# A gated state-space block and a ternary MLP on one core: in VectorE's order the gated chunk of an MLP tile goes behind the scan of its slot

## The chip, the cores and the metric

The kernel runs on one core of a Trainium2 chip. The metric is device time in microseconds, of one launch from start to end. Below, PE is the matrix engine (TensorE), DVE is VectorE, ACT is ScalarE, POOL is GpSimd and SP is the engine that only issues DMAs here. Each engine works through its own list of instructions in the order in which they are written; between engines the order is kept by semaphores alone.

## The reference, cut to what matters

The input x has 4 batches of 512 rows of 512 numbers. Two blocks follow one another, both with a residual.

1. A state-space block. A projection of a context, a convolution along time and a projection give, for each of 512 channels d, inputs `u`, step sizes `dt` (softplus), and for 16 states rows `B` and `C`. The recurrence is `state = state * exp(dt * A) + (dt * u) * B` along the 512 time steps, and `y = sum over states of state * C + D * u`. Then `y` is multiplied by `silu` of the normalised x, scaled, and added to x.
2. A ternary MLP on the normalised result: `h = silu(x w1) * (x w2)`, `out = h w3`, in which each product takes activations quantised row by row to 8 bits (after a division by their root mean square) and weights rounded to -1, 0 and 1. Hidden width 2048. The result is scaled and added.

The loop at issue works on both blocks at once: it scans the states of one batch while the MLP works on rows that are already finished.

## The kernel before, in words

**The scan pipeline.** The work on the states is cut into 128 steps k: 4 batches, 32 steps each, and in each step 1024 columns for 128 channels (two states of 512 time steps, or, in batches 2 and 3, four states of 256 time steps). A step passes five stations:

- POOL multiplies `dt * u` by the rows of B into a buffer `hh[k % 6]` (`times_b`, L702 or L708).
- ACT makes `exp(dt * A)` into the PSUM pair `dbank[k % 2]` (`exp`, L736 or L743).
- DVE scans (`scan`, L773, or four pieces with a carried state, L770).
- POOL multiplies the states by the rows of C, in place (`times_c`, L813 or L818). In 11 steps (the list `BY_VECTOR`) DVE does this (L796).
- PE turns the result and adds it into the bank `bank_y` (`sums`, L851), which frees `hh[k % 6]` for step k + 6.

Slot k of the loop is written out per engine: in slot k POOL does `times_c(k)` and `times_b(k + 4)`, ACT `exp(k + 4)`, DVE `scan(k + 3)`, PE `sums(k - 1)`. `times_b(k + 4)` waits until PE has done `sums(k - 2)`. Every eighth slot (40, 48, ..., 120) a bank of y is complete, and DVE does `gate` (L576, and L585 or L591): it multiplies `bank_y` by the gate and adds x. `gate` in slot k waits for `sums(k - 1)`.

**The MLP between.** 16 tiles of 128 rows. Tile i starts in slot T = `TILE[i]`, most of them 6 slots apart (38, 44, 50, 56, 70, 76, 82, 88, 94, 100, 106, 112, 118 for the 13 tiles inside the loops), and has four chunks c of 512 hidden columns:

- PE in slot T + c: `a_tensor` (L1020) into `bank_a`, then `b_tensor` (L1029) into `bank_b`, four products each. There is one bank of either kind, so the products of chunk c wait until DVE has read the banks of chunk c - 1 (L1018 and L1027).
- ACT in slot T + c + 1: `tanh_scalar` (L1041) of the first bank, ahead of the slot's `exp`.
- DVE in slot T + c + 1: `gated_vector`, two instructions: (tanh + 1) times `bank_a` (L1048, marked `g`), and that times `bank_b` (L1054, marked `h`).
- ACT in slots T + 2 and T + 4: `square_scalar` (L1059 to L1068), waits for `h` of chunks 1 and 3. DVE in the same slots: `peak_vector` (L1093), the largest magnitude of two chunks.
- Later: scales (L1106 to L1116), quantising on ACT, turning on PE, and in slot T + 10 the third product (`out_tensor`, L1211, 16 products) and DVE's `out_vector` (L1218), which adds it to the rows and lets SP store them. With tiles 6 slots apart, slot T + 10 of one tile is slot T + 4 of the next.

**The gate's own input.** `silu` of the normalised x is made in `z_scalar` on ACT (L523 and L524, in two halves for batches 2 and 3) and `z_vector` on DVE (L530), in the slots 42, 48, 54, 68, 74, 80, 86, 98, 104, 110 and 117 (`z_slot`). `z_scalar` uses `bank_a` and waits for `g` of chunk 3 of the tile before; it stands behind `square_scalar` in ACT's list. Nine of these slots (all but 68 and 117) are slot T + 4 of a tile.

**The two loops.** DVE's list is written by a loop over slots 38 to 79 (L1868) and another over 80 to 124 (L1910). Their orders in a slot, before the change: in the first, scales of a tile (L1871), `gated_vector`, `gate`, `scan`, the product by C where it is DVE's, and the rest; in the second, scales, `gate`, statistics of finished rows, `gated_vector`, `scan`, and the rest. In both, `peak_vector`, `out_vector` and `z_vector` come behind, in this order.

Of the kernel before, what the change touches and what calls it, by code (L numbers as in the profile page):

```python
# [25 lines left out]
STEPS = NS // GN  # L26
PER = NE * STEPS
ALL = NB * PER
NH = 6
LEAD = 4  # L30
# [63 lines left out]
def build(nc, book, x, ctx_t, in_w, xp_w, dt_w, weights, consts, out):  # L94
    u_dram = nc.dram_tensor("u_scratch", [NB, P, NE, L], F32).ap()
    xd_dram = nc.dram_tensor("xd_scratch", [NB, ROWS, L], F32).ap()
    with ExitStack() as ctx:
# [474 lines left out]
        def gate(v, g):  # L572
            b, q = g // NE, g % NE
            v.wait_ge(s_sum, STEPS * (g + 1))
            v.wait_ge(*ZA.of(("gT", g)))
            YV.did(v.tensor_tensor(bank_y[:, :], bank_y[:, :], gbuf[:, q, :], ALU.mult))  # L576
            if b in SPLIT:
                h, p = q // 2, q % 2
                if p == 0:
                    for t in (2 * h, 2 * h + 1):  # L580
                        v.wait_ge(*d_out[t].of(NE * (b - 2) + t))
                v.wait_ge(*YV.now())
                to, rows = [of[:, 2 * h:2 * h + 2, 2 * p * P:2 * (p + 1) * P].rearrange("p c (j d) -> p j c d", j=2)
                            for of in (x2[b % 2], xin)]
                YV.did(v.tensor_tensor(to, bank_y[:, :].rearrange("p (j c d) -> p j c d", j=2, c=2), rows, ALU.add),  # L585
                       ("y", g))
                return
            if g == NE:
                v.wait_ge(*WA.of(("sign", NW - 1)))
            v.wait_ge(*YV.now())  # L590
            YV.did(v.tensor_tensor(columns(x2[b % 2], q), by_rows(bank_y[:, :]), columns(xin, q), ALU.add), ("y", g))  # L591
# [166 lines left out]
        def scan(v, k):  # L758
            if k < 2:
                v.wait_ge(*BV.of(2 * k + 1))  # L760
            else:
                v.wait_ge(s_m1, m1_done(k))
            v.wait_ge(s_exp, k + 1)
            h, da = flat(hh[k % NH]), flat(dbank[k % 2])
            to = da if c_by_vector(k) else h
            if split(k) and where_split(k)[1]:
                b, _, q, n = where_split(k)
                for j in range(4):
                    t = slice(HALF * j, HALF * (j + 1))
                    ins = v.tensor_tensor_scan(to[:, t], da[:, t], h[:, t], hl[:, q, n + j:n + j + 1],  # L770
                                               ALU.mult, ALU.add)
            else:
                ins = v.tensor_tensor_scan(to, da, h, 0.0, ALU.mult, ALU.add)  # L773
            ins.then_inc(s_scan, 1)
# [324 lines left out]
        def scales_vector(v, i, part):  # L1099
            t = i % NE  # L1100
            if part == 0:
                v.wait_ge(*MV.of(("peak", i, NCH - 1 if at_end(i) else 1)))
                if at_end(i):
                    MV.did(v.tensor_scalar(am1, amh[:, 0:1], amh[:, 1:2], amh[:, 2:3], ALU.max, ALU.max))
                else:
                    MV.did(v.tensor_scalar(am1, amh[:, 0:1], amh[:, 1:2], None, ALU.max))  # L1106
                v.wait_ge(*MV.now())
                MV.did(v.reciprocal(ram1, am1))
            if part == 1:
                v.wait_ge(*MG.of(("rh", i)))  # L1110
                v.wait_ge(*MV.now())
                MV.did(v.tensor_scalar(rk_most, rh, kk[:, t:t + 1], 127e5, ALU.mult, ALU.mult))
                MV.did(v.tensor_scalar(rk_am, rh, kk[:, t:t + 1], am1, ALU.mult, ALU.mult))
                v.wait_ge(*MV.now())
                MV.did(v.tensor_scalar(csh, ram1, 127.0, rk_most, ALU.mult, ALU.min), ("csh", i))
                MV.did(v.tensor_scalar(fin[i % 2], rk_am, 1e-5, g3d, ALU.max, ALU.mult), ("fin", i))  # L1116
                v.wait_ge(*MV.now())
# [111 lines left out]
        with nc.Block() as block:  # L1229
# [556 lines left out]
            def _(v):  # L1786
# [81 lines left out]
                for k in range(38, 80):  # L1868
                    for i in range(END):
                        if k == tile_slot(i) + 7:  # L1870
                            scales_vector(v, i, 1)  # L1871
                    for i in range(END):
                        c = k - tile_slot(i) - 1
                        if 0 <= c < NCH:
                            gated_vector(v, i, c)
                    if k % STEPS == 0 and PER < k <= ALL:
                        gate(v, k // STEPS - 1)
                    if k + LEAD - 1 < ALL:
                        scan(v, k + LEAD - 1)
                    if k + LEAD - 1 < ALL and c_by_vector(k + LEAD - 1):  # L1880
                        times_c_vector(v, k + LEAD - 1)
                    for first, n, done in TURNS:
                        if k == done + 3:
                            rows_vector(v, first, n)
                    for i in range(END):
                        if k == tile_slot(i) + 5:
                            scales_vector(v, i, 0)
                    for first, n, done in TURNS:
                        if k == done + 2:
                            for i in range(first, first + n):  # L1890
                                stats_vector(v, i)
                            for i in range(first, first + n):
                                aggr_vector(v, i)
                    for i in range(END):
                        if k == tile_slot(i) + 4:
                            peak_vector(v, i, 1)
                    for i in range(END - 1):
                        if k == tile_slot(i) + 10:
                            out_vector(v, i)
                    for i in TILES:  # L1900
                        if k == z_slot(i):
                            z_vector(v, i)
                    for n in PAIR:
                        if k == PAIR[n]:
                            du_vector(v, 2 * n)
                            du_vector(v, 2 * n + 1)
                    for i in range(END):
                        if k == tile_slot(i) + 2:
                            peak_vector(v, i, 0)
                for k in range(80, SLOTS):  # L1910
                    for i in range(END):
                        if k == tile_slot(i) + 7:
                            scales_vector(v, i, 1)
                    if k % STEPS == 0 and PER < k <= ALL:
                        gate(v, k // STEPS - 1)
                    for first, n, done in TURNS:
                        if k == done + 2:
                            for i in range(first, first + n):
                                stats_vector(v, i)
                            for i in range(first, first + n):  # L1920
                                aggr_vector(v, i)
                    for i in range(END):
                        c = k - tile_slot(i) - 1
                        if 0 <= c < NCH:
                            gated_vector(v, i, c)
                    if k + LEAD - 1 < ALL:
                        scan(v, k + LEAD - 1)
                    for i in range(END):
                        if k == tile_slot(i) + 5:
                            scales_vector(v, i, 0)  # L1930
                    for first, n, done in TURNS:
                        if k == done + 3:
                            rows_vector(v, first, n)
                    for i in range(END):
                        if k == tile_slot(i) + 4:
                            peak_vector(v, i, 1)
                    for i in range(END):
                        if k == tile_slot(i) + 2:
                            peak_vector(v, i, 0)
                    for i in range(END - 1):  # L1940
                        if k == tile_slot(i) + 10:
                            out_vector(v, i)
                    for i in TILES:
                        if k == z_slot(i):
                            z_vector(v, i)
                    for n in PAIR:
                        if k == PAIR[n]:
                            du_vector(v, 2 * n)
                            du_vector(v, 2 * n + 1)
                    if k + LEAD - 1 < ALL and c_by_vector(k + LEAD - 1):  # L1950
                        times_c_vector(v, k + LEAD - 1)
# [81 lines left out]
```

## Time and profile before

| | |
|---|---|
| median of 3 runs | 653.23 us (653.22 to 656.8) |
| profiled execution | 653.69 us, span 651.9 us |
| PE busy, instructions | 488.3 us (75%), 2560 |
| DVE busy, instructions | 583.0 us (89%), 772 |
| ACT busy, instructions | 530.7 us (81%), 969 |
| POOL busy, instructions | 587.9 us (90%), 289 |
| mean granted PE clock | 0.897 of full speed |
| chain that ended last | POOL 30%, DVE 29%, ACT 14%, issue 13%, PE 11%, DMA 2% |

The span is the time from the first to the last instruction of the profiled execution; its own time is 1.8 us longer. Busy shares are means over the whole span, in which the loop with MLP tiles runs from about 215 us to about 605 us. The chain that ended last is followed back from the last instruction: at each step to what released it, or to the instruction before it on its engine. "Issue" is time in which the engine waited for nothing that the profile shows.

### The profile page before, as it was taken

What the parts mean: (1) busy time and instruction counts of PE and PEld (TensorE: products, weight loads), DVE (VectorE), ACT (ScalarE), POOL (GpSimd) and SP (SyncE); (2) the same over time, 40 slices, a digit from 0 to 9 for tenths busy, and PEclk for the clock granted to TensorE, in tenths of its full rate; (3) what the DMA queues carried; (4) which work ended last, traced back from release to release, by engine and by line L of the source; (5) the groups of instructions that cost most, each with busy time, mean ns of one, the idle gap of its engine ahead of it and who ended that gap; (6) DMA issues with size and microseconds to landing.
All of it is one profiled execution on the core that took longest, in us unless ns stands there. A gap on an engine that the chain in (4) does not pass through costs nothing.

```text
span 651.9 us, 7928 instructions
## 1 busy us (share of the span) xinstructions
PE 488.3 (75%) x2560; PEld 296.4 (45%) x2560; DVE 583.0 (89%) x772; ACT 530.7 (81%) x969; POOL 587.9 (90%) x289
## 2 busy tenths in 40 slices
PE   8798878994564678777666486778676887668987
PEld 3254434552553445455534354455454554345543
DVE  6779779997998899999999999989997999999765
ACT  5764767788999778987798797899999898897675
POOL 1399999998999999999999999999999999999431
PEclk9988999997555979999786889889989897978999
DMA  5598587579960100147420100037700000000001
GB/s 186 193 407 309 183 329 276 198 270 389 374 262 0 39 1 2 47 153 276 132 78 0 33 2 17 1 127 244 254 37 1 17 1 18 0 16 18 1 17 48
DMA packets 24472, 80.77 MB, mean 124 GB/s; under 512 B 2464, under 2 KB 5152, under 8 KB 21360
## 3 DMA queue, kind: packets, MB, share of 16 engines
q1 hardware_dynamic: 24432, 80.27, 33.9%
q8 instruction: 20, 0.33, 0.2%
q14 instruction: 20, 0.16, 0.1%
HBM read 72.53 MB, written 7.73 MB: 123 GB/s over the span
## 4 chain that ended last, share of the span: by engine, by line
POOL 30%; DVE 29%; ACT 14%; issue 13%; PE 11%; DMA 2%; SPq 0%; DVEq 0%; POOLq 0%; ACTq 0%
POOL hh L708 15%; POOL hh L818 14%; DVE hh L773 9%; DVE hh L770 8%; DVE room L1048 4%; ACT da L736 3%; DVE sm L1093 2%; PE bank_a L1020 2%; PE bank_b L1029 2%; PE bank_y L851 2%; ACT room L1041 1%; PE da L1211 1%; DVE bank_y L576 1%; DVE sm L904 1%; ACT gbuf L922 1%
## 5 line engine op out<-in xcount | busy, mean ns | idle before, releaser
L773 DVE TENSOR_TENSOR_SCAN hh<-da,hh 128x1024 f32<-128x1024 f32 x85 | 193.4, 2280 | 3.1 <-ACT da L743 3.0
L851 PE MATMUL bank_y<-ident,hh 128*128 128x128 f32 x1024 | 145.3, 292 | 10.8 <-POOL hh L818 8.8
L851 PEld LDWEIGHTS bank_y<-ident,hh 128*128 128x128 f32 x1024 | 129.6, 152 | 40.1 <-issue 17.5
L813 POOL TENSOR_TENSOR hh<-hh,cc 128x1024 f32<-128x1024 f32 x60 | 141.0, 2350 | 0.2 <-ACT hl L756 0.2
L818 POOL TENSOR_TENSOR hh<-hh,cc 128x1024 f32<-128x1024 f32 x57 | 134.2, 2355 | 0.0
L708 POOL TENSOR_TENSOR hh<-pair,bb 128x1024 f32<-128x1024 f32 x30 | 70.5, 2352 | 26.4 <-DMA bb<-xd_scratch 24.2
L770 DVE TENSOR_TENSOR_SCAN hh<-da,hl,hh 128x256 f32<-128x256 f32 x128 | 85.4, 729 | 0.0
L708 POOL TENSOR_TENSOR hh<-wq,bb 128x1024 f32<-128x1024 f32 x32 | 75.3, 2357 | 1.8 <-PE bank_y L851 1.8
L702 POOL TENSOR_TENSOR hh<-wq,bb 128x1024 f32<-128x1024 f32 x32 | 75.1, 2346 | 0.3 <-PE bank_y L851 0.3
L702 POOL TENSOR_TENSOR hh<-pair,bb 128x1024 f32<-128x1024 f32 x32 | 75.2, 2355 | 0.0
L736 ACT ACTIVATE da<-wq,cst 128x256 f32<-128x256 f32 x128 | 53.3, 463 | 12.0 <-DVE hh L770 11.6
L743 ACT ACTIVATE da<-pair,cst 128x511 f32<-128x511 f32 x64 | 41.3, 679 | 23.3 <-DVE hh L773 23.3
L1020 PE MATMUL bank_a<-wq,room 128*128 128x512 fp8e4 x120 | 34.2, 412 | 30.2 <-DVE room L1048 27.4
L736 ACT ACTIVATE da<-pair,cst 128x255 f32<-128x255 f32 x128 | 53.0, 459 | 3.5 <-DVE hh L773 3.4
L743 ACT ACTIVATE da<-wq,cst 128x511 f32<-128x511 f32 x64 | 41.4, 682 | 9.4 <-DVE hh L773 9.2
L1020 PE MATMUL bank_a<-wq,xqT 128*128 128x512 fp8e4 x112 | 32.4, 417 | 21.7 <-DVE room L1048 21.7
L1041 ACT ACTIVATE room<-bank_a,sm 128x512 f32<-128x512 f32 x58 | 39.0, 673 | 9.0 <-PE bank_a L1020 8.9
L1211 PE MATMUL bank_t<-wq,room 128*128 128x512 fp8e4 x192 | 45.0, 389 | 0.1
L1048 DVE SCALAR_TENSOR_TENSOR room<-room,bank_a 128x512 f32<-128x512 f32 x52 | 35.2, 677 | 8.0 <-ACT room L1041 7.6
L1029 PE MATMUL bank_b<-wq,room 128*128 128x512 fp8e4 x120 | 34.1, 411 | 0.0
L1190 ACT ACTIVATE room<-bank_t,sm 128x1024 bf16<-128x1024 f16 (+1 forms) x28 | 30.4, 1085 | 4.4 <-PE bank_t L1173 4.4
L987 PE MATMUL bank_t<-ident,room 128*128 128x128 f16 x56 | 6.1, 238 | 34.2 <-ACT room L969 17.4
(271 smaller groups left out, 1051.7 us busy)
## 6 DMA issues: line engine op xcount, KB each, us to landing
bb<-xd_scratch SPq DMA_DIRECT2D x32, 512.0 KB, 5.1
cc<-xd_scratch SPq DMA_DIRECT2D x32, 512.0 KB, 6.9
wq<-weights SPq DMA_DIRECT2D x12, 1024.0 KB, 6.5
stage<-weights SPq DMA_DIRECT2D x8, 1024.0 KB, 6.1
xin<-x SPq DMA_DIRECT2D x4, 1024.0 KB, 5.4
room<-weights SPq DMA_DIRECT2D x4, 1024.0 KB, 8.2
u_scratch<-wq SPq DMA_DIRECT2D x6, 512.0 KB, 3.0
wq<-x SPq DMA_DIRECT2D x2, 1024.0 KB, 18.8
```

Source lines behind the costliest of these rows:

```text
L702: ins = g_.tensor_tensor(quarters(flat(hh[k % NH])), du2[g % 4][:, HALF * (q % 2):HALF * (q % 2 + 1)].unsqueeze(1).to_broadcast([P, 4, HAL ...
L708: ins = g_.tensor_tensor(hh[k % NH][:, :, :], du2[g % 4].unsqueeze(1).to_broadcast([P, GN, L]), bb[:, s * GN:(s + 1) * GN, :], ALU.mult)
L736: ins = act.activation(da[:, j, first:HALF], dt2[g % 4][:, HALF * (q % 2) + first:HALF * (q % 2 + 1)], ACT.Exp, scale=a_neg[:, q, n + j:n ...
L743: ins = act.activation(dbank[k % 2][:, j, 1:L], dt2[g % 4][:, 1:L], ACT.Exp, scale=a_neg[:, q, s * GN + j:s * GN + j + 1])
L770: ins = v.tensor_tensor_scan(to[:, t], da[:, t], h[:, t], hl[:, q, n + j:n + j + 1], ALU.mult, ALU.add)
L773: ins = v.tensor_tensor_scan(to, da, h, 0.0, ALU.mult, ALU.add)
L813: ins = g_.tensor_tensor(quarters(flat(hh[k % NH])), quarters(flat(hh[k % NH])), cc[:, n:n + 4, t], ALU.mult)
L818: ins = g_.tensor_tensor(hh[k % NH][:, :, :], hh[k % NH][:, :, :], cc[:, s * GN:(s + 1) * GN, :], ALU.mult)
L851: mm = pe.matmul(bank_y[:, (first + c) * P:(first + c + 1) * P], flat(hh[k % NH])[:, at:at + P], ident[:, :], start=False, stop=(s == STEP ...
L1020: mm = pe.matmul(a[:, :], xqT[i % 2][:, k, :], w1q[:, k, c * 512:(c + 1) * 512], start=(k == 0), stop=(k == NE - 1))
L1048: MV.did(v.scalar_tensor_tensor(out=th[c % 2], in0=th[c % 2], scalar=1.0, in1=a[:, :], op0=ALU.add, op1=ALU.mult), ("g", i, c))
L1211: mm = pe.matmul(bank_g(i)[:, :], hqT[:, f, :], w3q[:, f, :], start=(f == 0), stop=(f == KF - 1))
```

## The change

In both loops of DVE's list the call of `scan` goes ahead of the call of `gated_vector`. In the first loop it takes `gate` along, which stood between the two. No instruction is added or removed, and the lists of the other engines are as before.

```diff
@@ -1869,14 +1869,14 @@  for k in range(38, 80)
                     for i in range(END):
                         if k == tile_slot(i) + 7:
                             scales_vector(v, i, 1)
+                    if k % STEPS == 0 and PER < k <= ALL:
+                        gate(v, k // STEPS - 1)
+                    if k + LEAD - 1 < ALL:
+                        scan(v, k + LEAD - 1)
                     for i in range(END):
                         c = k - tile_slot(i) - 1
                         if 0 <= c < NCH:
                             gated_vector(v, i, c)
-                    if k % STEPS == 0 and PER < k <= ALL:
-                        gate(v, k // STEPS - 1)
-                    if k + LEAD - 1 < ALL:
-                        scan(v, k + LEAD - 1)
                     if k + LEAD - 1 < ALL and c_by_vector(k + LEAD - 1):
                         times_c_vector(v, k + LEAD - 1)
...
@@ -1919,12 +1919,12 @@  for k in range(80, SLOTS)
+                    if k + LEAD - 1 < ALL:
+                        scan(v, k + LEAD - 1)
                     for i in range(END):
                         c = k - tile_slot(i) - 1
                         if 0 <= c < NCH:
                             gated_vector(v, i, c)
-                    if k + LEAD - 1 < ALL:
-                        scan(v, k + LEAD - 1)
```

## Rows read from the trace of the kernel before

**Rows 1.** Busy time by engine in two stretches (us and instructions), granted clock, DMA.
```profile
215.00:410.00 195.00, 136.17 (x830) 89.75 (x829) 186.91 (x219) 163.27 (x317) 194.72 (x91) 0.89 0.19 64
410.00:605.00 195.00, 145.49 (x890) 95.12 (x889) 184.20 (x281) 173.17 (x357) 194.75 (x92) 0.92 0.18 61
```

**Rows 2.** Waits of POOL, 215 to 605 us: total us, times, longest.
```profile
POOL hh L702 <- PE bank_y L851: 0.3, 1, 0.3
POOL hh L813 <- ACT hl L756: 0.2, 1, 0.2
```

**Rows 3.** Waits of DVE, 215 to 605 us.
```profile
DVE room L1048 <- ACT room L1041: 7.6, 8, 2.4
...
DVE gbuf L530 <- ACT bank_a L524: 0.9, 3, 0.5
...
DVE bank_y L576 <- PE bank_y L851: 0.7, 1, 0.7
```

**Rows 4.** Groups by line, 215 to 605 us: busy us, mean ns.
```profile
L773 DVE TENSOR_TENSOR_SCAN hh<-da,hh 128x1024 f32<-128x1024 f32 x46 | 105.0, 2282 | 0.1
...
L770 DVE TENSOR_TENSOR_SCAN hh<-da,hl,hh 128x256 f32<-128x256 f32 x128 | 85.4, 729 | 0.0
```

**Rows 5.** Timeline of slots 103 and 104: start us, us, engine, line, operation.
```profile
504.99 0.69 DVE L1048 SCALAR_TENSOR_TENSOR room<-room,bank_a 128x512 f32<-128x512 f32 x1
...
505.74 1.04 PE L1020 MATMUL bank_a<-wq,xqT 128*128 128x512 fp8e4 x4 [1.50 <-DVE room L1048]
506.32 2.28 DVE L773 TENSOR_TENSOR_SCAN hh<-da,hh 128x1024 f32<-128x1024 f32 x1
...
506.61 1.03 PE L1029 MATMUL bank_b<-wq,xqT 128*128 128x512 fp8e4 x4
507.47 1.04 PE L851 MATMUL bank_y<-ident,hh 128*128 128x128 f32 x8
...
508.35 3.62 PE L1211 MATMUL bank_t<-wq,room 128*128 128x512 fp8e4 x16
508.55 0.70 DVE L576 TENSOR_TENSOR bank_y<-bank_y,gbuf 128x512 f32<-128x512 f32 x1
...
509.99 0.68 DVE L1048 SCALAR_TENSOR_TENSOR room<-room,bank_a 128x512 f32<-128x512 f32 x1
...
510.70 0.69 DVE L1054 TENSOR_TENSOR wq<-room,bank_b 128x512 f32<-128x512 f32 x1
511.31 2.28 DVE L773 TENSOR_TENSOR_SCAN hh<-da,hh 128x1024 f32<-128x1024 f32 x1
511.42 1.06 ACT L1059 ACTIVATE room<-wq 128x1024 f32<-128x1024 f32 x1 [0.28 <-DVE wq L1054]
...
513.51 1.19 DVE L1093 TENSOR_REDUCE sm<-wq 128x1 f32<-128x1024 f32 x1
...
514.38 0.55 ACT L524 ACTIVATE bank_a<-xin,sm 128x256 f32<-128x256 f32 x1
514.62 0.74 DVE L1218 SCALAR_TENSOR_TENSOR room<-bank_t,sm,room 128x512 f32<-128x512 f32 x1
...
515.27 0.68 DVE L530 SCALAR_TENSOR_TENSOR gbuf<-bank_a,gbuf 128x512 f32<-128x512 f32 x1
```

**Rows 6.** Timeline, the gate of slot 120; in brackets the idle time before it.
```profile
582.79 0.70 DVE L576 TENSOR_TENSOR bank_y<-bank_y,gbuf 128x512 f32<-128x512 f32 x1 [0.70 <-PE bank_y L851]
```

**Rows 7.** Timeline, the last scan and POOL's last two products by C.
```profile
601.69 2.67 DVE L770 TENSOR_TENSOR_SCAN hh<-da,hl,hh 128x256 f32<-128x256 f32 x4
...
602.99 4.67 POOL L813 TENSOR_TENSOR hh<-hh,cc 128x1024 f32<-128x1024 f32 x2
```

**Rows 8.** Timeline, PE's first and second products of a chunk in slot 124.
```profile
600.67 1.91 PE L1020 MATMUL bank_a<-wq,xqT 128*128 128x512 fp8e4 x4
...
602.38 1.32 PE L1029 MATMUL bank_b<-wq,xqT 128*128 128x512 fp8e4 x4
```

**Rows 9.** Busy time by engine and granted clock (after POOL), the stretch of rows 8.
```profile
600.00:603.60 3.60, 3.60 (x14) 1.83 (x13) 3.57 (x8) 2.11 (x3) 3.60 (x4) 0.59 0.12 46
```

## The prediction

> **What bounds the kernel now.** I read first the busy time by engine in the stretch with MLP tiles, cut in two. Both halves show the same: POOL is busy for 389.5 of 390 us, DVE for 371.1; PE and ACT have 50 us and more to spare [rows 1]. Then I asked each of the two what it waits for. POOL waits 0.5 us in all, so it has no gap that a better order could close [rows 2]. DVE waits little and mostly in one place: eight times for a tanh, 7.6 us together [rows 3]; that is what a scan put ahead of the gated chunk can cover. The two engines are level: at the end of the loop the last scan is over at 601.69 + 2.67 = 604.36, and POOL takes its product up behind the one before, at 602.99 + 4.67 / 2 = 605.33 [rows 7]. So DVE has 0.97 us to spare against POOL, and all that it loses beyond this, and doesn't win back, moves the end.
>
> Last I followed, in one worked pair of slots (103 and 104, tile 9), what leaves a gated chunk and comes back to DVE [rows 5]. Three things do.
>
> - To the next gate. The first gated instruction (g) ends at 505.68; PE starts the next chunk's products at 505.74, the second four at 506.61, the sums at 507.47, done at 508.51; the gate starts at 508.55. That is 2.87 us behind the end of g. DVE was busy all the while, with the second gated instruction (h) and the scan. In slot 120 even that isn't enough: the gate waits 0.70 us for the sums [rows 6].
> - To z. ACT's square waits for h of chunk 3 (over at 511.39), starts at 511.42, z is done at 514.38 + 0.55 = 514.93: 3.54 us behind h. DVE has scan, peak and out between, and takes z up at 515.27, with 0.34 us to spare. Elsewhere this spare is already gone (three waits, 0.9 us) [rows 3].
> - To out. The sixteen products of the third weight stand on PE behind the last chunk's, and are done at 508.35 + 3.62 = 511.97, 6.29 us behind the end of g.
>
> **The change part by part.** It adds and removes no instruction, DMA or semaphore; only DVE's order changes, in the 52 slots with a chunk. Each engine's queue but DVE's keeps its order, SP's too: its stores follow out, its loads the same marks. DVE's busy time stays, so the sum is one of waits.
>
> *Gates.* Behind the change g and h of slot k - 1 come behind that slot's scan, and the gate follows at once: the order is scan, g, h, gate. h ends 0.64 us behind g (pair of 1.33 us, 504.99 to 506.32, less g's 0.69 [rows 5]). The gate's sums are still 2.87 us behind g. So DVE stands still for 2.87 - 0.64 = 2.23 us. In the first loop the gate used to stand behind another gated pair of its own slot; that goes behind it too, so no cover is left there either. It concerns the gates whose sums follow a chunk's products that wait for g: slots 40, 48, 72, 80, 96, 104 and 120 (slot T + 2 or T + 4 of a tile), not 56, 64, 88 and 112. Seven times 2.23, less the 0.70 that slot 120 waits already: 14.9 us. Behind the waiting gate stand the slot's scan, and behind that ACT's next exp and POOL's product by C. Bounds: none if sums came early (nothing in PE's order lets them), and twice as much at a slower PE (below).
>
> *z.* The order in slot T + 4 becomes scan, g, h, peak, out, z. Behind h there are only peak and out, 514.62 - 513.51 = 1.11 and 515.27 - 514.62 = 0.65 us [rows 5], against ACT's 3.54: a wait of 1.8 us. So in slots 80, 86, 98, 104 and 110: 8.9 us. In the four others (42, 48, 54, 74) z is in one piece, or a product by C stands between; I take 1.1 us each, an estimate between none and 1.8: 4.4 us.
>
> *out.* Where out comes in slot T + 4 without a z (60, 92, 116, 122), DVE gets there 0.64 + scan + 1.33 + 1.11 us behind g of chunk 2: 5.36 with a scan of 2.28, 5.75 with one of 2.67 [rows 4, 7]. The products need 6.29. Waits of 0.9 and three times 0.5: 2.5 us.
>
> *Tanh.* The scan now covers the waits for it: back come up to 7.6 us [rows 3]. I take all of it; the lower bound is nothing.
>
> *POOL's other product.* The product by B waits for sums of two slots before, and these for the chunk's products, which now come a scan (2.28 us) later. POOL waited 0.3 us there once [rows 2], so its spare was nil in one slot; by itself this costs at most 2.3 us, once, since a shift of POOL makes the next ones fit. It lies beside DVE's delay, which is longer: nothing in the sum.
>
> *exp.* Tanh stands ahead of exp in ACT's list and waits for a later g, by up to one scan. From the end of g it takes at most 1.1 us for PE's products, and 1.1 and 2.2 us for tanh (512 columns) and exp (1024), by z's 0.55 us for 256 [rows 5]: 4.4 us, an upper end, since pieces on ACT overlap a little. DVE needs h, a scan and the next pair, 0.64 + 2.28 + 1.33 = 4.25 us, before it asks for that exp. Level at worst, so nothing in the sum; if it isn't hidden, see the rivals.
>
> Sum: 14.9 + 8.9 + 4.4 + 2.5 - 7.6 = 23.1, less the spare of 0.97: 22.1 us. On the profiled execution's 653.69 this is 675.8; it lies 0.5 above the median, so 675.4 us.
>
> The lengths on PE are those of its faster clock: the step from one group of four products to the next is 0.87 us in rows 5, and 602.38 - 600.67 = 1.71 us where the granted clock was 0.59 in a stretch that holds both levels, 1.2 and 2.4 GHz [rows 8, 9]. The Trainium skill (TensorE: Matmul & The Clock Gate, "Part 1: The HAM clock gate") says that the half rate is the default state and that idle lets the engine fall back to it. By it the longer waits of PE for g would lower the clock further; the trace so far has 0.89 and 0.92 in the two halves, with such waits of 1.50 us in rows 5. The sum by that rule is a rival's.
>
> **The rivals.**
>
> - *POOL alone counts (not slower).* For it: POOL's 0.5 us of gaps against DVE's 18.9 (390 - 371.1) of idle [rows 1, 2]. If DVE could make up what it loses at gates and z before its products are wanted, only the one shift of POOL remained: 2.3 us, so 655.5 us. It decides if new waits of DVE stay below 7.6 + 0.97 us. Against it: the 0.97 us at the end [rows 7].
> - *Waits covered (faster).* If sums, z and out are hidden after all, 7.6 us of DVE's are free; POOL can give back only its 0.5 us, so 652.7 us, no measurable change. A gain over 1% would have to come out of the tail, whose order isn't touched.
> - *PE falls to its half rate.* Place: the products between g and the gate. Price: two steps of 1.71 in place of 0.87 [rows 5, 8], and about as much for out and sums, 2 us at each of seven gates: 14 us more, 690 us.
> - *exp comes late.* If ACT's list is so full that exp ends 1 us behind DVE in each of 13 tiles: 13 us more, 688 us.
>
> **How the numbers follow.** Within 1% (646.7 to 660) is about what can't be told from no change. The forecast has 0.67, between 662 (z hidden, 13.3 us less) and 683 (the tanh waits stay, 7.6 us more) as its own range; half rate 0.09; late exp 0.08; POOL alone 0.12; faster by over 1% 0.04, for what I don't see. The range 661 to 690 holds the forecast's cases and about half of the two slower ones. Slower by over 1%: 0.67 + 0.09 + 0.08 = 0.84; within 1%: 0.12; faster: 0.04.
>
> **What would show it.** In the profile after: the gates of the seven slots idle about 2.2 us for PE's sums, z in nine slots idle for ACT's tanh of z, up to 1.8 us; the waits of g for tanh nearly gone; POOL no longer without gaps, but idle some 20 us, most of it before products by B, for PE's sums. DVE's busy time is as before, and the tail behind POOL's last product as long. The prediction is wrong if the gates wait and the end doesn't move (then DVE had spare time that I don't see), or if the gates don't wait (then sums aren't bound to g), or if scans wait for exp.

## The result and the profile after

The changed kernel takes 690.5 us (median of 4 runs, 690.23 to 691.75), the one before 653.23 us (4 runs, 652.93 to 656.8): a ratio of 1.0539, 95% interval 1.0506 to 1.0572, so about 37 us slower. The prediction said 675.4 us: the direction is right, the loss was 37 us in place of 22, and 690.5 lies just outside the range. The profiled execution has a span of 688.4 us, 36.5 more than before, at a mean granted clock of 0.873.

Busy time by engine in the stretch with MLP tiles comes first, up to 0.6 us behind the last scan as in [rows 1] (us from and to, length, PE, PE's loads, DVE, ACT, POOL, granted clock, DMA share, GB/s):

```profile
215.00:428.00 213.00, 145.67 (x822) 95.20 (x820) 186.75 (x217) 161.53 (x315) 195.79 (x92) 0.84 0.17 59
428.00:640.80 212.80, 153.06 (x895) 97.65 (x896) 187.59 (x283) 175.00 (x359) 192.91 (x91) 0.89 0.16 56
```

The stretch has grown from 390 to 425.8 us. DVE is busy for 374.3 us of it (371.1 before) and idle for 51.5 (18.9 before); POOL, which had no gap, is idle for 37.1. So both engines that were level before stand still now. Which of them makes the other wait is read from their waits. DVE's (the form of [rows 3]):

```profile
DVE bank_y L576 <- PE bank_y L851: 17.6, 7, 4.7
DVE gbuf L530 <- ACT bank_a L524: 13.6, 10, 2.1
DVE stage L1218 <- PE bank_t L1211: 2.4, 3, 1.5
DVE room L1048 <- ACT room L1041: 2.3, 4, 0.8
DVE sm L1112 <- POOL sm L1127: 2.1, 3, 1.4
DVE hh L773 <- ACT da L743: 2.1, 2, 1.2
DVE room L1218 <- PE bank_t L1211: 1.4, 2, 0.9
```

The waits for tanh are down from 7.6 to 2.3 us; in their place stand gate (0.7 before, now 17.6), z (0.9, now 13.6) and out (none, now 2.4 + 1.4). POOL's waits (of [rows 2], 0.5 us in all):

```profile
POOL hh L702 <- PE bank_y L851: 22.5, 6, 5.5
POOL hh L708 <- PE bank_y L851: 11.7, 4, 4.7
POOL hh L813 <- ACT hl L756: 2.7, 2, 1.5
```

Products by B wait for sums, 34.2 us. That alone doesn't tell cause from consequence: sums wait on PE behind the chunk's products, these wait for DVE's g. Now the same tile and slots as [rows 5] in the timeline (start us, us, engine, line, operation; in brackets the idle time before it and what ended it), and behind them the gate of slot 120 [rows 6] and the end of the loop [rows 7]:

```profile
531.78 2.28 DVE L773 TENSOR_TENSOR_SCAN hh<-da,hh 128x1024 f32<-128x1024 f32 x1
...
533.97 0.66 DVE L1048 SCALAR_TENSOR_TENSOR room<-room,bank_a 128x512 f32<-128x512 f32 x1
...
534.67 0.69 DVE L1054 TENSOR_TENSOR wq<-room,bank_b 128x512 f32<-128x512 f32 x1
...
534.69 1.04 PE L1020 MATMUL bank_a<-wq,xqT 128*128 128x512 fp8e4 x4 [1.53 <-DVE room L1048]
...
536.43 1.04 PE L851 MATMUL bank_y<-ident,hh 128*128 128x128 f32 x8
...
537.50 0.70 DVE L576 TENSOR_TENSOR bank_y<-bank_y,gbuf 128x512 f32<-128x512 f32 x1 [2.15 <-PE bank_y L851]
...
541.84 0.69 DVE L1054 TENSOR_TENSOR wq<-room,bank_b 128x512 f32<-128x512 f32 x1
542.56 1.06 ACT L1059 ACTIVATE room<-wq 128x1024 f32<-128x1024 f32 x1 [2.98 <-DVE wq L1054]
542.56 1.22 DVE L1093 TENSOR_REDUCE sm<-wq 128x1 f32<-128x1024 f32 x1
...
543.70 0.74 DVE L1218 SCALAR_TENSOR_TENSOR room<-bank_t,sm,room 128x512 f32<-128x512 f32 x1
...
546.11 0.69 DVE L530 SCALAR_TENSOR_TENSOR gbuf<-bank_a,gbuf 128x512 f32<-128x512 f32 x1 [1.67 <-ACT bank_a L524]
...
617.31 0.70 DVE L576 TENSOR_TENSOR bank_y<-bank_y,gbuf 128x512 f32<-128x512 f32 x1 [2.15 <-PE bank_y L851]
...
637.47 2.67 DVE L770 TENSOR_TENSOR_SCAN hh<-da,hl,hh 128x256 f32<-128x256 f32 x4
...
639.53 4.69 POOL L813 TENSOR_TENSOR hh<-hh,cc 128x1024 f32<-128x1024 f32 x2
```

From the end of g (533.97 + 0.66 = 534.63) to the gate it is 2.87 us, to the hundredth what it was. The way back hasn't grown; what changed is that DVE has only h to do meanwhile, and so stands for 2.15 us. In slot T + 4 the same: h ends at 542.53, peak and out follow, and z stands for 1.67 us. The last scan ends at 640.14, 35.8 us later than before. POOL takes its last product up at about 639.53 + 4.69 / 2 = 641.9 (605.33 before) and is done with it at 644.2, 36.5 later, as much as the span. The tail behind it is as long as before.

One gate is unlike the others, that of slot 96:

```profile
487.92 1.89 PE L1020 MATMUL bank_a<-wq,room 128*128 128x512 fp8e4 x4 [4.42 <-DVE room L1048]
489.60 1.91 PE L1029 MATMUL bank_b<-wq,room 128*128 128x512 fp8e4 x4
491.31 1.91 PE L851 MATMUL bank_y<-ident,hh 128*128 128x128 f32 x8
...
493.26 0.70 DVE L576 TENSOR_TENSOR bank_y<-bank_y,gbuf 128x512 f32<-128x512 f32 x1 [4.67 <-PE bank_y L851]
```

PE had stood still for 4.42 us; its steps, from one group of products to the next, are 1.68 and 1.71 us long here in place of 0.87, as in [rows 8], and the gate waits 4.67 us. The granted clock of that stretch (columns as above) is 0.57, near the lower of the two levels, 1.2 of 2.4 GHz:

```profile
486.00:494.00 8.00, 5.81 (x24) 3.42 (x24) 3.26 (x5) 5.54 (x12) 8.00 (x5) 0.57 0.50 186
```

### The profile page after: what moved, and what is told of

Read it like the earlier page. It is cut to its first block, busy times and chain, and to the rows that moved or that the text cites. A ratio compares the mean times of both kernels' runs of the same rounds, so it can differ in the third digit from the quotient of the medians.

```text
span 688.4 us, 7917 instructions
## 1 busy us (share of the span) xinstructions
PE 505.5 (73%) x2560; PEld 304.5 (44%) x2560; DVE 586.4 (85%) x772; ACT 531.6 (77%) x969; POOL 588.3 (85%) x289
## 4 chain that ended last, share of the span: by engine, by line
DVE 36%; PE 20%; ACT 19%; issue 13%; POOL 5%; DMA 4%; SPq 2%; DVEq 0%; ACTq 0%; POOLq 0%
DVE hh L773 10%; DVE hh L770 8%; DVE room L1048 4%; PE bank_a L1020 3%; PE bank_y L851 3%; PE bank_b L1029 3%; DMA wq<-x 2%; ACT da L743 2%; DVE da L773 2%; ACT da L736 2%; POOL hh L813 2%; ACT room L1059 2%; DVE wq L1054 2%; PE bank_b L256 1%; ACT gbuf L523 1%
## 5 line engine op out<-in xcount | busy, mean ns | idle before, releaser
L851 PE MATMUL bank_y<-ident,hh 128*128 128x128 f32 x1024 | 147.8, 295 | 10.3 <-POOL hh L818 7.0
L851 PEld LDWEIGHTS bank_y<-ident,hh 128*128 128x128 f32 x1024 | 132.5, 155 | 41.6 <-issue 20.4
L1020 PE MATMUL bank_a<-wq,room 128*128 128x512 fp8e4 x120 | 39.4, 461 | 45.1 <-DVE room L1048 40.9
L1020 PE MATMUL bank_a<-wq,xqT 128*128 128x512 fp8e4 x112 | 34.7, 440 | 28.5 <-DVE room L1048 28.5
L1211 PE MATMUL bank_t<-wq,room 128*128 128x512 fp8e4 x192 | 43.4, 379 | 0.1
L1190 ACT ACTIVATE room<-bank_t,sm 128x1024 bf16<-128x1024 f16 (+1 forms) x28 | 30.6, 1094 | 16.6 <-PE bank_t L1173 16.6
L1029 PE MATMUL bank_b<-wq,room 128*128 128x512 fp8e4 x120 | 39.5, 462 | 0.0
L1020 PEld LDWEIGHTS bank_a<-wq,room 128*128 128x128 bf16 x120 | 11.5, 110 | 59.5 <-DVE room L1048 44.4
```

What stands on the lines that cost most here:

```text
L851: mm = pe.matmul(bank_y[:, (first + c) * P:(first + c + 1) * P], flat(hh[k % NH])[:, at:at + P], ident[:, :], start=False, stop=(s == STEP ...
L1020: mm = pe.matmul(a[:, :], xqT[i % 2][:, k, :], w1q[:, k, c * 512:(c + 1) * 512], start=(k == 0), stop=(k == NE - 1))
L1029: mm = pe.matmul(b_[:, :], xqT[i % 2][:, k, :], w2q[:, k, c * 512:(c + 1) * 512], start=(k == 0), stop=(k == NE - 1))
```

## The experiments

Two theories are told apart. **D**: DVE's own waits (gate, z, out) set the end, and POOL's are what follows from them. **P**: the sums that come a scan later starve POOL of free buffers, and POOL's waits set the end. The kernel before was timed beside each kernel: 654.54 us (7 runs) with the first four, 655.55 us (7 runs) with the last three. "Last scan" is its end in the profiled execution, whose waits in the loop are given, in us.

| kernel | median us (range) | ratio, 95% interval | last scan | gate | z | tanh | out |
|---|---|---|---|---|---|---|---|
| before | 653.23 | 1 | 604.36 | 0.7 | 0.9 | 7.6 | 0 |
| changed | 690.5 (690.23 to 691.75) | 1.0539 (1.0506 to 1.0572) | 640.14 | 17.6 | 13.6 | 2.3 | 3.8 |
| changed, gate behind scan | 671.69 (669.91 to 672.95) | 1.0247 (1.0194 to 1.0299) | 622.89 | 3.3 | 13.5 | 1.1 | 2.3 |
| changed, chunk 3 ahead | 683.03 (680.81 to 685.0) | 1.0428 (1.0379 to 1.0477) | 631.47 | 19.1 | 0.9 | 12.7 | 0 |
| both of these | 670.13 (666.5 to 671.37) | 1.0223 (1.0172 to 1.0274) | 620.86 | 2.8 | 0.7 | 18.2 | 0 |
| changed, POOL lighter | 687.1 (685.43 to 689.75) | 1.0495 (1.0447 to 1.0543) | 637.64 | 16.7 | 12.9 | 3.1 | 3.3 |
| before, chunk 3 behind | 673.94 (672.05 to 675.52) | 1.0286 (1.0258 to 1.0314) | 622.72 | 1.8 | 14.3 | 7.4 | 0 |
| before, seven chunks behind | 672.98 (672.57 to 674.84) | 1.027 (1.0246 to 1.0294) | 625.49 | 22.2 | 0.9 | 4.7 | 0 |
| gate behind scan, z a slot later | 669.61 (667.37 to 671.68) | 1.022 (1.0186 to 1.0255) | 618.32 | 5.7 | 5.7 | 0.8 | 2.8 |

**The changed kernel, gates behind the scans too.** If the gate is given a scan to wait behind, its stall should go, and POOL's waits with it under D.

```diff
-                    if k % STEPS == 0 and PER < k <= ALL:
-                        gate(v, k // STEPS - 1)
...
                     if k + LEAD - 1 < ALL:
                         scan(v, k + LEAD - 1)
+                    if k % STEPS == 0 and PER < k <= ALL:
+                        gate(v, k // STEPS - 1)
                     for i in range(END):
                         c = k - tile_slot(i) - 1
```

> The changed kernel (690.5 us) with one thing more: gate stands behind the scan of its slot, ahead of the gated chunk, in both loops. Theory D (the loss is DVE's waits, one after the other on its own list): the 17.6 us that seven gates wait for PE's sums go, because a scan of 2.28 us covers 2.23; the waits of z and out stay. 673 us, between 669 and 677. Rival P (the loss is POOL's 34 us of waits for sums ahead of its products by B, since every chunk's products on PE come a scan later): the chunks come as late as before, so 687 to 691 us.

Measured: 671.69 us, as D has it. Half of the loss is the gates. In the waits, gate falls from 17.6 to 3.3 us (two gates, with PE's products partly at the half rate), z stays at 13.5, and POOL's waits for sums fall from 34.2 to 16.4 us, though no chunk has gone back ahead of its scan:

```profile
DVE gbuf L530 <- ACT bank_a L524: 13.5, 10, 1.8
DVE bank_y L576 <- PE bank_y L851: 3.3, 2, 1.6
...
POOL hh L702 <- PE bank_y L851: 9.2, 7, 2.7
POOL hh L708 <- PE bank_y L851: 7.2, 3, 5.6
```

**The changed kernel, chunk 3 back ahead of the scan.** Chunk 3 alone sends z off, so z should be covered again. The edit is the same in both loops.

```diff
+                    for i in range(END):
+                        c = k - tile_slot(i) - 1
+                        if 0 <= c < NCH and c == 3:
+                            gated_vector(v, i, c)
                     if k + LEAD - 1 < ALL:
                         scan(v, k + LEAD - 1)
                     for i in range(END):
                         c = k - tile_slot(i) - 1
-                        if 0 <= c < NCH:
+                        if 0 <= c < NCH and c < 3:
                             gated_vector(v, i, c)
```

> The changed kernel (690.5 us) with chunk 3 of each tile ahead of the scan of its slot, as it was before the change; chunks 0 to 2 stay behind it, and gate ahead. Theory D: the 13.6 us that z waits and the 3.8 us that out waits go, the gates' 17.6 stay: 674 us, between 670 and 678. Rival P: no products of the same tile wait for chunk 3, so POOL's sums come as late as in the changed kernel: 687 to 691 us.

Measured: 683.03 us, 5 us above D's range and 4 us below P's. z is covered (13.6 to 0.9 us), but the waits for tanh went from 2.3 to 12.7 us. The timeline of slots 85 and 86 shows why:

```profile
436.81 0.66 DVE L1048 SCALAR_TENSOR_TENSOR room<-room,bank_a 128x512 f32<-128x512 f32 x1
...
437.51 0.69 DVE L1054 TENSOR_TENSOR room<-room,bank_b 128x512 f32<-128x512 f32 x1
437.53 1.04 PE L1020 MATMUL bank_a<-wq,room 128*128 128x512 fp8e4 x4 [1.91 <-DVE room L1048]
...
438.80 0.67 ACT L1041 ACTIVATE room<-bank_a,sm 128x512 f32<-128x512 f32 x1
...
439.51 0.69 DVE L1048 SCALAR_TENSOR_TENSOR room<-room,bank_a 128x512 f32<-128x512 f32 x1 [1.31 <-ACT room L1041]
```

Chunk 2 is behind its scan and chunk 3 ahead of the next, so no scan lies between the two g's. The first ends at 437.47, its tanh is back at 439.47, and h alone doesn't fill that. D as I had put it, gate and z by themselves, was too narrow: tanh is a fourth return that needs a scan of its own.

**Both of these edits.** The order is chunk 3, scan, gate, chunks 0 to 2.

> Both edits together: chunks 0 to 2 behind the scan, chunk 3 ahead, gate behind the scan. Theory D: the savings add, 17 and 17 us: 656 us, between 651 and 662, near the kernel before (653.2), with most of the 7.6 us of tanh waits gone and POOL back as what bounds, with waits of at most a few us. Rival P: chunks 0 to 2 are as late as in the changed kernel, so 684 to 691 us.

Measured: 670.13 us, in neither range: 8 us above D's and 14 us below P's. Gate (2.8) and z (0.7) are covered, and tanh waits 18.2 us, fifteen times. With gates and z both repaired the kernel is no better than with the gates alone: the last scan comes 16.5 us later than in the kernel before, and 10.6 us of that are the tanh waits beyond its 7.6.

**The changed kernel with a lighter POOL.** Half of each product by C is left out on POOL from step 40 on, so the states of the other half aren't multiplied.

```diff
-                ins = g_.tensor_tensor(quarters(flat(hh[k % NH])), quarters(flat(hh[k % NH])), cc[:, n:n + 4, t],
-                                       ALU.mult)
+                ins = g_.tensor_tensor(quarters(flat(hh[k % NH]))[:, 0:2, :], quarters(flat(hh[k % NH]))[:, 0:2, :],
+                                       cc[:, n:n + 2, t], ALU.mult)
...
-                ins = g_.tensor_tensor(hh[k % NH][:, :, :], hh[k % NH][:, :, :], cc[:, s * GN:(s + 1) * GN, :],
+                m = 1 if k >= 40 else GN
+                ins = g_.tensor_tensor(hh[k % NH][:, 0:m, :], hh[k % NH][:, 0:m, :], cc[:, s * GN:s * GN + m, :],
```

> The changed kernel, and POOL's product by C is made for half of the columns only from step 40 on, half of the states' products by C being left out (the output is not the reference's): POOL has some 78 times 1.2 us = 93 us less to do. Theory D: DVE's waits for gate, z and out don't hang on POOL, so they stay, and the time falls by no more than 4 us: 686 to 690.5 us. Rival P: POOL makes up its 34 us of waits in its free time, so the time comes back to about the kernel before or below, 640 to 660 us.

Measured: 687.1 us, with POOL's busy time down from 588.3 to 503.4 us. DVE's waits hardly move (table); POOL only waits longer for the same sums (lines 1 higher):

```profile
POOL hh L702 <- PE bank_y L852: 72.1, 36, 7.1
POOL hh L708 <- PE bank_y L852: 29.6, 9, 6.9
```

85 us of work taken from POOL bring 3.4 us. So POOL's work isn't what the end waits for. Nor do its waits hold DVE up: in none of the nine profiles does a scan wait for POOL, so the products by B, late as they are, still come ahead of the scans that need them. P is refuted for the loop, and POOL's waits there are a consequence; on the last 17 us, in which POOL's list ends the kernel, see the spare of 0.97 us in the next section.

**The kernel before with only chunk 3 behind its scan.** The converse of the second experiment: one part of the change done alone, in both loops.

```diff
-                        if 0 <= c < NCH:
+                        if 0 <= c < NCH and c < 3:
                             gated_vector(v, i, c)
...
                         scan(v, k + LEAD - 1)
+                    for i in range(END):
+                        c = k - tile_slot(i) - 1
+                        if 0 <= c < NCH and c == 3:
+                            gated_vector(v, i, c)
```

> The kernel before, with only chunk 3 of every tile behind the scan of its slot; chunks 0 to 2 and the gates stay where they were. Theory D (VectorE's own waits set the end, each return needs a scan between it and the instruction that sends it off): behind h of chunk 3 there is no scan any more, so z waits as in the changed kernel, 12.7 us more, and the gates stay covered. out hangs on g of chunk 3 as far as its products stand on TensorE behind that chunk's: up to 3.8 us. No gate waits beyond the 0.7 us of slot 120. 653.2 + 12.7 + 3.8 = 669.7, less up to 1 us of spare: 669 us (665 to 673), z waits of 11 to 14 us. Rival P (it is GpSimd's waits for sums that set the end; chunk 3 has no products of its own tile queued behind it on TensorE, so the sums come nearly as early as before): 653 to 656 us.

Measured: 673.94 us, D's side, 1 us above its range. The z waits are all there, 14.3 us against 13.6 in the changed kernel:

```profile
DVE gbuf L530 <- ACT bank_a L524: 14.3, 10, 1.8
...
DVE bank_y L576 <- PE bank_y L851: 1.8, 2, 1.5
```

out doesn't wait at all (up to 3.8 expected): its products follow g of chunk 2, which hasn't moved, so the expectation had the wrong chunk. One gate waits 1.46 us, with its sums at the half rate. In this profiled execution DVE was 1.6 us later than before already at about 201 us, ahead of the loop that the edit touches; that is part of the overshoot (1.9 us in the next experiment, too).

**The kernel before with seven chunks behind their scans.** Only the chunks one slot ahead of a gate (slots 39, 47, 71, 79, 95, 103, 119) are moved; in the first loop the gate stands ahead of its own slot's chunk, as in the second.

```diff
-                        if 0 <= c < NCH:
+                        if 0 <= c < NCH and (k + 1) % STEPS:
                             gated_vector(v, i, c)
...
                         scan(v, k + LEAD - 1)
+                    for i in range(END):
+                        c = k - tile_slot(i) - 1
+                        if 0 <= c < NCH and not (k + 1) % STEPS:
+                            gated_vector(v, i, c)
```

> The kernel before, with only seven of the 52 chunks behind their scans: those of slots 39, 47, 71, 79, 95, 103 and 119, one slot ahead of a gate; in the first loop the gate stands ahead of the chunk of its own slot, as in the second, so that no cover is left there. Theory D: seven gates wait 2.15 to 2.23 us as in the changed kernel, 14.9 us more than before; the waits for tanh that these seven chunks had fall away (up to 2 us), and behind each such chunk stands the waiting gate, which covers the next tanh. 653.2 + 14.9 less 1 to 2: 667 us (663 to 671), gate waits of 13 to 17 us. Rival P (GpSimd's waits for sums set the end): seven sums are late by one scan, but the shift of GpSimd by one of them makes the next fit, so 655 to 658 us.

Measured: 672.98 us, P refuted again and D's range overshot by 2 us. The gates wait 22.2 us, not 15: three of the seven 2.15 us, the other four 3.71, 3.83, 3.82 and 4.38. Slot 40 shows what these have:

```profile
220.66 1.04 PE L1020 MATMUL bank_a<-wq,room 128*128 128x512 fp8e4 x4 [3.12 <-DVE room L1048]
221.53 1.76 PE L1029 MATMUL bank_b<-wq,room 128*128 128x512 fp8e4 x4
...
223.08 1.91 PE L851 MATMUL bank_y<-ident,hh 128*128 128x128 f32 x8
225.03 0.70 DVE L576 TENSOR_TENSOR bank_y<-bank_y,gbuf 128x512 f32<-128x512 f32 x1 [3.71 <-PE bank_y L851]
```

PE's rate fell in the middle of the chunk, from a step of 0.87 us to one of 1.55, and the sums took 1.91 us in place of 1.04. The other three chunks with such a gate stood behind 4.87, 4.36 and 4.33 us of idle on PE; the three whose gate waits 2.15 us stood behind 1.91 us at most. The seven chunks alone cost half of what all 52 do.

**Gates behind the scans, and six of z a slot later.** The first experiment's kernel, with DVE's part of z in slots 42, 54, 74, 80, 104 and 110 put behind the next slot's scan and gate (its lines are 3 higher).

```diff
+        def z_late(i):
+            return z_slot(i) in (42, 54, 74, 80, 104, 110)
...
                     if k % STEPS == 0 and PER < k <= ALL:
                         gate(v, k // STEPS - 1)
+                    for i in TILES:
+                        if k == z_slot(i) + 1 and z_late(i):
+                            z_vector(v, i)
...
-                        if k == z_slot(i):
+                        if k == z_slot(i) and not z_late(i):
                             z_vector(v, i)
```

> The changed kernel with the gates put behind the scans as well (the kernel that took 671.7 us), and of z's eleven slots six (42, 54, 74, 80, 104, 110) with VectorE's part of z one slot later, behind that slot's scan and gate. Theory D: in these six slots the waits of z go (8.4 us there: 0.75, 1.10, 1.54 and three of 1.66), the other z waits stay (about 5 us), nothing else is late: 671.7 - 8.4 = 663 us (659 to 667). Rival (what VectorE gains there it loses at the next wait, since GpSimd or the chunks' products are late too): unchanged, 670 to 673 us.

Measured: 669.61 us, between the two expectations, and by its interval not apart from the kernel it builds on. The profiled executions say what happened: the six waits went (z 13.5 to 5.7 us) and the last scan came 4.6 us earlier, not 8, since other waits came up:

```profile
DVE gbuf L533 <- ACT bank_a L527: 5.7, 4, 1.8
DVE bank_y L579 <- PE bank_y L854: 5.7, 3, 2.5
DVE sm L1115 <- POOL sm L1130: 3.7, 3, 2.1
```

Gates have 2.4 us more (slot 96 at the half rate for all its products), the scales behind POOL 1.4, out 0.5. No kernel of these beats the one before.

## Why the prediction was right in direction and too small

By the steps of the prediction, with the waits of the profile:

- **What bounds the kernel, and that DVE's delay moves the end: right.** The last scan moved by 35.8 us, DVE's idle time by 51.5 - 18.9 = 32.6 and its busy time by 3.2, which is that sum. The lighter POOL, and that no scan waits for POOL, show that it is DVE's list and not POOL.
- **Gates: 14.9 forecast, 17.6 - 0.7 = 16.9 measured.** All seven wait, at the slots named. Six wait 2.15 us (2.23 forecast: I took the scan's start at 506.32 for h's end, and h ends 0.08 later); slot 96 waits 4.67, 2.5 us for the half rate.
- **z: 13.3 forecast, 13.6 - 0.9 = 12.7 measured. out: 2.5 forecast, 3.8 measured.** Together 15.8 and 16.5. The split was off: of the four slots named for out only 92 and 122 wait; in slots 86, 98 and 110 out waits first and so takes part of z's wait, slot 74 waits 2.14 where I took 1.1, and slot 117, which I left out, waits 1.84.
- **Tanh: 7.6 back forecast, 5.3 measured**; four waits are left.
- **Put at nothing, and not nothing.** exp: two scans of the first loop wait for it, 2.1 us, which the prediction had named as a sign of being wrong. I had reckoned it level at 4.4 against 4.25 us and taken zero, from PE's products, tanh and exp alone. Neither wait comes from these three alone. The first is in slot 39, where g waited 2.35 us for tanh before; its exp stands on ACT behind the load of a function table and ahead of the tanh. At the second ACT has another activation of 1.11 us (L1190) between tanh and exp:

```profile
213.10 1.28 ACT L743 ACT_TABLE_LOAD   x1
...
215.80 2.29 DVE L773 TENSOR_TENSOR_SCAN hh<-da,hh 128x1024 f32<-128x1024 f32 x1 [1.25 <-ACT da L743]
...
289.32 1.11 ACT L1190 ACTIVATE room<-bank_t,sm 128x1024 bf16<-128x1024 f16 x1
...
291.73 2.29 DVE L773 TENSOR_TENSOR_SCAN hh<-da,hh 128x1024 f32<-128x1024 f32 x1 [0.86 <-ACT da L743]
```

- **Other waits put at nothing.** Scales (L1112) wait for POOL 1.0 us more, the softplus chunks (L353) 1.4 us more. With exp's 2.1 these are 4.5 us; with the 3.2 of busy time they are the larger part of the miss.
- **Busy time as before: wrong by 3.2 us**, with as many instructions. The last section shows where the larger part of it comes from.
- **The spare of 0.97 us: not used.** POOL now takes its last product up 1.7 us behind the end of the last scan instead of 0.97, so DVE's delay counts in full, and 0.8 us more come from POOL. It waits 5.0 us for sums here and then has no gap until 644.2, so in these last 17 us POOL's list ends the kernel:

```profile
627.46 2.35 POOL L702 TENSOR_TENSOR hh<-wq,bb 128x1024 f32<-128x1024 f32 x1 [5.03 <-PE bank_y L851]
```

- **POOL's idle time: 20 us forecast, 37 measured**, before products by B as said.

The sum by measured terms: 16.9 + 12.7 + 3.8 - 5.3 + 2.1 + 1.0 + 1.4 = 32.6 us of waits, + 3.2 busy = 35.8, + 0.8 at the end = 36.6 of the span's 36.5. Two small items that nearly cancel are left out: 0.5 us of waits for `bank_b` that went, and some 0.7 us of gaps between neighbours (last section). The forecast's own four terms make 28.1 where it said 23.1: tanh 2.3, gates 2.0 and out with z 0.7. The step that failed is "DVE's busy time stays, so the sum is one of waits" together with the waits put at nothing (exp, scales, softplus) and the spare: 3.2 + 4.5 + 0.97 + 0.8 = 9.5 of the missing 36.6 - 22.1 = 14.5 us; the other 5.0 are the four terms'.

Of the rivals, "waits covered" and "POOL alone counts" are refuted. "PE falls to its half rate" came true at one gate of seven, 2.5 us and not 14, in the profiled execution; in the experiment with seven chunks at four of seven, 22.2 - 7 x 2.15 = 7.2 us. The Trainium skill (TensorE: Matmul & The Clock Gate, "Part 1: The HAM clock gate") says that the half rate is the default state, to which idle lets the engine fall back: by that rule a stall of DVE's can make PE slow just for the work it waits for. Slot 96, with 0.57 behind 4.42 us of idle, agrees; slot 40 of the changed kernel, which kept the full rate behind 3.12 us, shows that it can also go well. "exp comes late" was 2.1 us, not 13.

## What to carry to other kernels

An instruction that starts a trip through other engines wants work behind it on its own engine that is as long as the trip: here tanh is back 2 us, the gate's sums 2.9, z 3.5 and out 6.3 us behind it, and the order before had a scan of 2.3 us or more behind every chunk for that. Putting the long instruction ahead covers the one wait that is seen and uncovers those that were hidden, which no list of waits shows; so before a move, list every return with its length and with what lies in between. And give what comes out level (exp, by 0.15 us) or seems too small to count (overlaps of 0.08 us) a price of its own, with all that stands in the other engine's list in between: what the prediction put at nothing was 7.7 of the 36.5 us.

## What the runs showed of the hardware that was not expected

- **Neighbours on DVE overlap where the second doesn't wait for the first's result.** Before, the scan behind h starts at 511.31, 0.08 us before h ends (511.39) [rows 5]; after, peak, which reads what h writes, starts at 542.56, 0.03 us behind h's end (542.53). (The program also has such a second instruction wait by a semaphore; the runs don't separate the two.) After, peak stands right behind h 23 times, and before never: there it stood behind a scan or a product and overlapped. 23 times the lost 0.083 us is 1.9 of the 3.2 us of busy time, and 23 times the gap of 0.03 is 0.7 us of idle time. The rest of the 3.2 is spread over other neighbours and isn't split up here.
- **The same idle of PE, two rates.** In slot 40 PE waits 3.12 us for g both in the changed kernel and in that with seven chunks moved. In the one the two steps are 0.87 and 0.86 us long and the sums take 1.04; in the other the first step is 0.87, the second 1.55 and the sums take 1.91 (its rows stand with that experiment). The changed kernel:

```profile
218.73 1.04 PE L1020 MATMUL bank_a<-wq,room 128*128 128x512 fp8e4 x4 [3.12 <-DVE room L1048]
219.60 1.03 PE L1029 MATMUL bank_b<-wq,room 128*128 128x512 fp8e4 x4
...
220.46 1.04 PE L851 MATMUL bank_y<-ident,hh 128*128 128x128 f32 x8
221.54 0.70 DVE L576 TENSOR_TENSOR bank_y<-bank_y,gbuf 128x512 f32<-128x512 f32 x1 [2.15 <-PE bank_y L851]
```

The length of that gap doesn't decide by itself; what does wasn't separated here.
